# Attention with a feed-forward branch, float32, one core: a new order of each unit's work on TensorE, ScalarE and VectorE

## Chip, core and metric

The kernel runs on one core of a Trainium2 chip. The metric is the device time of one execution in microseconds, as a median of several. The engines are called by their short names in the rows: PE (TensorE; PEld is its weight load), ACT (ScalarE), DVE (VectorE), POOL (GpSimd) and SP (SyncE, which issues all DMAs here).

## What is computed

The input x is (4, 1024, 128) in float32. With xn the layer norm of x over the last axis, the result is x + attention(xn) + ffn(xn).

```python
# attention
xq, xk, xv = rope(xn @ Wq), rope(xn @ Wk), xn @ Wv      # 16 heads of 64; k and v have 512 columns
xk, xv = jnp.repeat(xk, 2, axis=-1), jnp.repeat(xv, 2, axis=-1)
scores = softmax(xq @ xk * scale, axis=-1)              # scale = (64 / 16) ** -0.5
out = (scores @ xv) @ Wo
# ffn
h = silu(xn @ wg.T) * (xn @ wu.T)                       # 384 hidden, integer weights / 127
out = h @ wd.T
```

Since each column of k and v is repeated, a head has 32 different ones (E = 32). The projection weights are drawn eight times larger than usual, so the scores are large and the softmax needs its row maximum.

## The kernel before

**Units.** A step is one batch and one group of four heads (16 steps, s), with a half of the 1024 queries as a unit: 32 units, u = 2s + t. Unit u computes 8 key tiles (kt) of 128 keys against 512 queries for 4 heads (h). The body `slot` (L544 on PE, L847 on ACT, L1051 on DVE, L1191 on POOL) is written out for units 0 to 30; the last unit has code of its own (`last_slot`). Units 28 to 30 (`last_pair`) project nothing any more.

**What one unit does.** All engines run their own list in order and meet at semaphores.

- Scores (`score`, L551 to 556): 32 matmuls, one for each kt and h, from `qk_pack` into `bank_s`, which has two places, by h % 2. ACT takes the exponential of each (L867) into `prob`, a ring of 4 key tiles. The row maximum is subtracted by two extra rows of `qk_pack` (98 rows instead of 96), so a unit's maxima must be known before it begins. Score (kt, h) waits until the exponential two scores back is done.
- Maxima (`max_tile`, L386): for the next unit v = u + 1, 16 tiles m of 128 queries; each is two matmuls of 512 columns (queries against all 1024 keys) into one of two places of the tensor `scores` (m % 2), and one maximum on DVE (`reduce_tile`, L943, L946). Tile m waits until DVE has read tile m - 2. After tile 15 DVE splits the maxima into two parts (`split_max`, L952 and L954), PE transposes them (`transpose_max`, L398), ACT copies them (`read_maxT`, L764), and SP's DMA (`pack_max`, L252) puts them into `qk_pack`; the next unit's first score waits for that (L582).
- V products (`pv`, L400 to L408): for each kt eight instructions in the profile, into four column strips of 32 of the array (`bank_o`). Before, they come in pairs of key tiles (`pv_pair`, L558): kt 6 and 7 of the unit before, then 0 and 1, 2 and 3, 4 and 5.
- Denominators: POOL adds the eight exponential tiles (L1173, L1181; tiles 4 and 5 are first added on DVE, `pair_sum`, L1039). PE sums over keys with a matrix of ones, also in column strips (`denominators`, L416 and L419), ACT copies (`read_den`, L834), PE transposes (`transpose_den`, L426), DVE inverts (`invert`, L1043), ACT spreads (`spread_inv`, L839), PE transposes back (`transpose_inv`, L433), DVE multiplies (`normalise`, L1049). All of it is for unit u - 1, and `project_out` (L442) for unit u - 2; `read_o` (L828) and `read_y` (L845) copy results out of PSUM.
- Projections for unit u + 4: four chunks c for q and k (`project`, L373, three matmuls each, into the same tensor `scores`; `project_chunk` waits for maxima that have been read) and V (`project_v`, L381, twelve matmuls into `bank_m`). DVE rotates the chunks (`rotate`, L937 to L941, six instructions); ACT rounds (`round_hi`, L753) and copies V (`stage_v`, L758); POOL takes the remainder (`split_lo`, L1125); SP packs heads with 24 DMAs a step (`pack_heads`, L239) and V with two (`pack_v`, L247), all in even units.

`bank_m` holds in turn the transposed maxima, V, the output product, the denominators and both transposes.

**The order around the change.** The order is written by hand in PE's `slot`: for each kt the scores h = 0 to 3 and between them the other work. `maxima()` takes the next tile of an iterator. On ACT the copies stand behind given exponentials (kt, h). On DVE `INVERT_AFTER` says after which maximum the inversion comes; the normalisation stands behind the split.

Of the kernel before, what the change touches and what calls it, by code (L numbers as in the profile page):

```python
# [39 lines left out]
UNITS = 2 * STEPS  # L40
HALF = S // 2

KT = S // 128
# [28 lines left out]
INVERT_AFTER = 9  # L72


def build(nc, x, tables, w_qkv, wo_even, wo_odd, w_gu, w_down, ident_in, out):
# [10 lines left out]
    with ctx:  # L86
# [272 lines left out]
        def _(pe):  # L359
# [184 lines left out]
            def slot(i, j, t, last_pair):  # L544
# [3 lines left out]
                do_max = not (last_pair and j == 1 and t == 1)  # L548
                tiles = iter(range(TILES))
# [8 lines left out]
                def pv_pair(kt):  # L558

                    if kt > 0:  # L560
                        pv(u, kt - 2, j)
                        pv(u, kt - 1, j)
                    elif not is_first(u):
                        pv(u - 1, KT - 2, j if t == 1 else 1 - j)
                        pv(u - 1, KT - 1, j if t == 1 else 1 - j)

                def maxima():
                    if do_max:
                        m = next(tiles)
                        if m < 2:  # L570

                            pe.wait_ge(rope_done, capped(2 * u + 7 + m, 2 * UNITS))
                        max_tile(v, m, v_n, v_t)
# [12 lines left out]
                if do_max and t == 1:  # L586

                    pe.wait_ge(packed, 16 * PACKS * (s + 1))
                for kt in range(KT):
                    score(kt, 0)  # L590
                    if kt == 0:
                        maxima()
                        score(kt, 1)
                        maxima()
                        score(kt, 2)
                        pv_pair(kt)
                        score(kt, 3)
                        maxima()
                    elif kt == 1:
                        maxima()  # L600
                        score(kt, 1)
                        if not is_second(u):
                            project_out(u - 2, 1 - j, s - 1)
                        score(kt, 2)
                        maxima()
                        score(kt, 3)
                    elif kt == 2:
                        maxima()
                        score(kt, 1)
                        maxima()  # L610
                        pv_pair(kt)
# [3 lines left out]
                        maxima()  # L615
                        score(kt, 3)
                        maxima()
                    elif kt == 3:
                        if not is_first(u):
                            transpose_den(u - 1)  # L620
                        score(kt, 1)
                        maxima()
                        score(kt, 2)
                        maxima()
                        score(kt, 3)
                    elif kt == 4:
                        maxima()
# [638 lines left out]
```

## Time and profile before

| | us |
|---|---|
| median of 3 runs | 1166.23 |
| the three runs | 1156.73, 1166.23, 1166.93 |
| the profiled execution | 1166.15 |
| its span, first to last instruction | 1164.4 |
| PE busy | 1120.0 (96%) |
| POOL busy | 852.9 (73%) |
| DVE busy | 901.1 (77%) |
| ACT busy | 729.8 (63%) |

The span is divided so: 110.7 us before the first unit, 31 units in the written-out body up to 1124.4, and the last unit. Matmuls are pipelined, so the recorded length of one is longer than what it takes of PE's time: the spacing from start to start tells that. A busy PE may thus be one that waits.

### The profile page before, as it was taken

The numbers are of one execution on the slowest core, as the hardware profiler recorded it, in microseconds if no ns is written. First come the engines' busy times: TensorE is split into PE (matmuls) and PEld (weight loads), VectorE is DVE, ScalarE is ACT, GpSimd is POOL, SyncE is SP. The second block draws the span as 40 slices with busy tenths as digits, with TensorE's granted clock in tenths as the row PEclk, the third lists the DMA queues.
The fourth block names the chain that finished last, engine by engine and source line by source line (L and its number), as shares of the span: only waits on it lengthen the run. The fifth ranks groups of instructions, "written<-read, shape, count | busy, mean of one in ns | idle before, by whom it ended". The sixth has DMA issues, their size and how long they took to land.

```text
span 1164.4 us, 17086 instructions
## 1 busy us (share of the span) xinstructions
PE 1120.0 (96%) x6288; PEld 663.2 (57%) x6288; DVE 901.1 (77%) x1023; ACT 729.8 (63%) x1327; POOL 852.9 (73%) x268
## 2 busy tenths in 40 slices
PE   5899899999999999999999999999999999999997
PEld 4787455655565555556565555555555555554443
DVE  7686877787887877788787877778787877776655
ACT  3234666666676666666676666666676666665564
POOL 3222868788788778888788778887778878887660
PEclk9899999999999999999999999999999999998889
DMA  6662908062340718062341718072341618050000
GB/s 230 159 258 77 256 2 224 1 205 58 85 141 19 207 37 224 2 205 57 96 129 26 201 37 224 1 210 53 96 130 30 196 37 224 1 130 1 5 1 19
DMA packets 56338, 124.98 MB, mean 107 GB/s; under 512 B 8000, under 2 KB 19520, under 8 KB 54080
## 3 DMA queue, kind: packets, MB, share of 16 engines
q1 hardware_dynamic: 56256, 123.90, 36.8%
q8 instruction: 51, 0.84, 0.3%
q14 instruction: 31, 0.25, 0.1%
HBM read 53.08 MB, written 10.49 MB: 55 GB/s over the span
## 4 chain that ended last, share of the span: by engine, by line
PE 79%; DVE 14%; SPq 2%; ACT 2%; issue 1%; DMA 1%; POOL 0%; DVEq 0%; ACTq 0%; POOLq 0%
PE bank_o L406 20%; PE bank_s L554 18%; PE scores L391 17%; DVE row_max L946 12%; PE scores L373 7%; PE bank_m L381 3%; PE bank_m L442 2%; PE bank_m L416 2%; PE bank_m L419 2%; SPq L239 2%; PE scores L492 2%; PE bank_s L509 1%; ACT prob L867 1%; PE bank_o L509 1%; DVE stats L961 1%
## 5 line engine op out<-in xcount | busy, mean ns | idle before, releaser
L946 DVE TENSOR_REDUCE row_max<-scores 128x1 f32<-128x1024 f32 x512 | 597.1, 1214 | 206.8 <-PE scores L391 206.5
L867 ACT ACTIVATE prob<-bank_s 128x512 f32<-128x512 f32 x992 | 576.7, 600 | 252.9 <-PE bank_s L554 229.5
L1181 POOL TENSOR_TENSOR prob_sum<-prob_sum,prob 128x2048 f32<-128x2048 f32 x93 | 425.7, 4577 | 13.5 <-ACT prob L867 0.5
L554 PE MATMUL bank_s<-qk_pack 98*128 98x512 f32 x992 | 415.8, 434 | 7.1 <-ACT prob L867 3.1
L391 PE MATMUL scores<-qk_pack 96*128 96x512 f32 x1024 | 337.5, 411 | 8.9 <-DVE row_max L946 0.3
L554 PEld LDWEIGHTS bank_s<-qk_pack 98*128 98x128 f32 x992 | 186.9, 189 | 184.9 <-issue 84.7
L406 PE MATMUL bank_o<-prob,v 128*32 128x512 f32 x2048 | 253.0, 612 | 0.0
L391 PEld LDWEIGHTS scores<-qk_pack 96*128 96x128 f32 x1024 | 179.5, 190 | 74.5 <-DVE row_max L946 53.0
L1181 POOL TENSOR_TENSOR prob_sum<-prob_sum,prob_pair 128x2048 f32<-128x2048 f32 x31 | 142.7, 4602 | 101.7 <-DVE prob_pair L1039 101.7
L1125 POOL TENSOR_TENSOR qk_stage<-rope,qk_stage 128x512 fp32r<-128x512 f32 x64 | 81.8, 1279 | 92.3 <-ACT qk_stage L753 92.3
L1173 POOL TENSOR_TENSOR prob_sum<-prob 128x2048 f32<-128x2048 f32 x31 | 142.2, 4586 | 0.0
L406 PEld LDWEIGHTS bank_o<-prob,v 128*32 128x32 f32 x2048 | 54.0, 110 | 123.1 <-issue 69.1
L373 PE MATMUL scores<-x_stage,w_stage 128*128 128x512 f32 x336 | 98.6, 401 | 0.0
L834 ACT COPY den<-bank_m 128x512 f32<-128x512 f32 x31 | 18.2, 586 | 86.6 <-PE bank_m L419 86.6
L1039 DVE TENSOR_TENSOR prob_pair<-prob 128x2048 f32<-128x2048 f32 x31 | 70.8, 2285 | 0.0
L373 PEld LDWEIGHTS scores<-x_stage,w_stage 128*128 128x128 f32 x336 | 61.4, 189 | 14.5
L1189 POOL TENSOR_TENSOR y_acc<-y_part,y_acc 128x512 f32<-128x512 f32 x31 | 39.5, 1274 | 26.5 <-ACT y_part L845 26.5
L381 PEld LDWEIGHTS bank_m<-w_stage,x_stage 128*128 128x128 f32 x336 | 46.3, 191 | 3.6
L937 DVE TENSOR_TENSOR scores<-scores,table 128x512 f32<-128x512 f32 x64 | 44.2, 691 | 2.5 <-PE scores L373 2.5
L941 DVE TENSOR_TENSOR rope<-scores,rope 128x512 f32<-128x512 f32 x64 | 44.3, 692 | 2.2
L939 DVE TENSOR_TENSOR rope<-scores,table 128x512 f32<-128x512 f32 x64 | 43.6, 681 | 0.6 <-PE scores L373 0.5
L381 PE MATMUL bank_m<-w_stage,x_stage 128*128 128x128 f32 x336 | 43.8, 266 | 0.0
(105 smaller groups left out, 742.4 us busy)
## 6 DMA issues: line engine op xcount, KB each, us to landing
qk_pack<-qk_stage SPq DMA_DIRECT2D x384, 128.0 KB, 5.0
table<-tables SPq DMA_DIRECT2D x16, 2048.0 KB, 9.6
w_stage<-w_scratch SPq DMA_DIRECT2D x14, 640.0 KB, 4.5
v<-v_stage SPq DMA_DIRECT2D x32, 256.0 KB, 8.1
xT_scratch<-xT_hl SPq DMA_DIRECT2D x4, 1024.0 KB, 9.5
x_stage<-xT_scratch SPq DMA_DIRECT2D x4, 1024.0 KB, 7.0
w_scratch<-w_split SPq DMA_DIRECT2D x1, 2560.0 KB, 15.1
x_all<-x SPq DMA_DIRECT2D x4, 512.0 KB, 11.7
```

The lines of the kernel that those rows point to most:

```text
L373: last = mm(scores[:, c, :], w_from[:, a, c, :], x_from[:, r, cols], start=n == 0, stop=n == 2)
L381: last = mm(bank_m[:, j * 128:(j + 1) * 128], x_from[:, r, at:at + 128], w_from[:, a, 4, :], start=n == 0, stop=n == 2)
L391: last = mm(scores[:, 2 * (m % places) + c, :], qk_pack[n][0:SPLIT_K, 0, t, h, (m % QT) * 128:(m % QT + 1) * 128], qk_pack[n][0:SPLIT_K, 1 ...
L406: last = mm(bank_o[h * E:(h + 1) * E, :], v_sb[n][:, kt, h * E:(h + 1) * E], prob[:, kt % RING, h, :], start=kt == 0, stop=kt == KT - 1)
L554: mm(bank_s[:, h % 2, :], qk_pack[j][0:SCORE_K, 1, kt // QT, h, (kt % QT) * 128:(kt % QT + 1) * 128], qk_pack[j][0:SCORE_K, 0, t, h, :], s ...
L867: A(prob[:, kt % RING, h, :], bank_s[:, h % 2, :], ACT.Exp).then_inc(prob_ready, 1)
L941: V.tensor_tensor(rope[:, 2 * k, :], scores[:, 2 * k, :], rope[:, 2 * k + 1, :], ALU.add).then_inc(rope_done, 1)
L946: V.tensor_reduce(row_max[:, m:m + 1], scores[:, at:at + 2, :].rearrange("p c k -> p (c k)"), axis=AX.X, op=ALU.max).then_inc(max_read, 1)
L1039: V.tensor_tensor(prob_pair[:], prob[:, 4 % RING], prob[:, 5 % RING], ALU.add).then_inc(pair_done, 1)
L1125: TT(qk_stage[:, 2 * k + 1, t, :], rope[:, 2 * k, :], qk_stage[:, 2 * k, t, :].bitcast(F32), ALU.subtract).then_inc(lo_done, 1)
L1173: TT(prob_sum[:, t], prob[:, 0], prob[:, 1], ALU.add).then_inc(sum_done, 1)
L1181: TT(prob_sum[:, t], prob_sum[:, t], part, ALU.add).then_inc(sum_done, 1)
```

## The change

The order of a unit is rewritten on PE, and the lists of ACT and DVE are set to suit. No matmul, exponential or maximum is added or left out.

- Maximum 0 of the next unit moves to the end of the present one (`next_first_maximum`), with the wait for the packed heads in front of it (`packed`, once in two units) and a wait for the rotation. The wait for `packed` at the head of odd units goes. The other 15 maxima have places named by number.
- The V products come as: kt 7 of the unit before (in kt 1), 0 and 1 together (kt 3), 2 (kt 4), 3 (kt 5), 4 to 6 together (kt 7). The denominators no longer follow a V product.
- `project_v` of unit u + 4: blocks 0 and 1 at the end of unit u, blocks 2 and 3 in kt 0 of unit u + 1 (`second_half_v`).
- The four chunks stand one between two scores in kt 6, and `transpose_max` behind them; it was between the first two.
- On ACT `round_hi`, `stage_v`, `read_o`, `read_den`, `spread_inv` and `read_maxT` move to other exponentials. On DVE the inversion comes after maximum 7 (before: 9) and the normalisation after maximum 14 (before: behind the split).
- The removed `do_max` was always true in the written-out body.

```diff
-INVERT_AFTER = 9
+INVERT_AFTER = 7
+NORMALISE_AFTER = 14
...
-                def pv_pair(kt):
-
-                    if kt > 0:
-                        pv(u, kt - 2, j)
-                        pv(u, kt - 1, j)
-                    elif not is_first(u):
-                        pv(u - 1, KT - 2, j if t == 1 else 1 - j)
+                def pv_last():
+                    if not is_first(u):
                         pv(u - 1, KT - 1, j if t == 1 else 1 - j)
...
+                def maximum(m):
+                    if m == 1:
+
+                        pe.wait_ge(rope_done, capped(2 * u + 8, 2 * UNITS))
+                    max_tile(v, m, v_n, v_t)
+
+                def next_first_maximum():
+                    if u + 2 <= LAST:
+
+                        pe.wait_ge(rope_done, capped(2 * u + 9, 2 * UNITS))
+                        if t == 0:
+                            pe.wait_ge(packed, 16 * PACKS * (s + 1))
+                        max_tile(u + 2, 0, 1 - j, t)
+
+                def second_half_v():
+                    if 1 <= u <= UNITS - 4:
+                        project_v(u + 3, 1 - t, blocks=range(QT // 2, QT))
...
-                if do_max and t == 1:
-
-                    pe.wait_ge(packed, 16 * PACKS * (s + 1))
                 for kt in range(KT):
                     score(kt, 0)
                     if kt == 0:
-                        maxima()
+                        if is_first(u):
+                            pe.wait_ge(rope_done, 7)
+                            max_tile(v, 0, v_n, v_t)
+                        maximum(1)
                         score(kt, 1)
-                        maxima()
+                        second_half_v()
                         score(kt, 2)
-                        pv_pair(kt)
+                        maximum(2)
                         score(kt, 3)
-                        maxima()
+                        maximum(3)
                     elif kt == 1:
-                        maxima()
+                        pv_last()
+                        maximum(4)
                         score(kt, 1)
+                        maximum(5)
+                        score(kt, 2)
                         if not is_second(u):
                             project_out(u - 2, 1 - j, s - 1)
-                        score(kt, 2)
-                        maxima()
                         score(kt, 3)
+                        maximum(6)
                     elif kt == 2:
-                        maxima()
+                        maximum(7)
                         score(kt, 1)
-                        maxima()
-                        pv_pair(kt)
                         if not is_first(u):
                             denominators(u - 1, 1 - t)
                         score(kt, 2)
-                        maxima()
                         score(kt, 3)
-                        maxima()
-                    elif kt == 3:
+                        maximum(8)
                         if not is_first(u):
                             transpose_den(u - 1)
+                        maximum(9)
+                    elif kt == 3:
                         score(kt, 1)
-                        maxima()
+                        pv(u, 0, j)
+                        pv(u, 1, j)
                         score(kt, 2)
-                        maxima()
                         score(kt, 3)
+                        maximum(10)
+                        maximum(11)
                     elif kt == 4:
-                        maxima()
                         score(kt, 1)
-                        pv_pair(kt)
+                        pv(u, 2, j)
                         score(kt, 2)
-                        maxima()
+                        maximum(12)
                         score(kt, 3)
-                        maxima()
+                        maximum(13)
                     elif kt == 5:
                         if not is_first(u):
                             transpose_inv(u - 1)
                         score(kt, 1)
-                        maxima()
+                        maximum(14)
                         score(kt, 2)
-                        maxima()
+                        pv(u, 3, j)
                         score(kt, 3)
+                        maximum(15)
                     elif kt == 6:
-                        pv_pair(kt)
+                        project_chunk(0)
                         score(kt, 1)
-                        project_chunk(0)
+                        project_chunk(1)
                         score(kt, 2)
...
-                        project_chunk(1)
+                        project_chunk(2)
                         score(kt, 3)
-                        project_chunk(2)
+                        project_chunk(3)
+
+                        at_least(pe, o_done, u)
+                        transpose_max(v)
                     else:
-                        project_chunk(3)
                         score(kt, 1)
+                        for n in (4, 5, 6):
+                            pv(u, n, j)
+                        score(kt, 2)
+                        score(kt, 3)
+                        next_first_maximum()
                         if not last_pair:
                             pe.wait_ge(maxT_read, v + 1)
                             project_v(w, t, blocks=range(QT // 2))
-                        score(kt, 2)
-                        if not last_pair:
-                            project_v(w, t, blocks=range(QT // 2, QT))
-                        score(kt, 3)
...
                     if kt == 1:
-                        pv(LAST - 1, KT - 2, 1)
                         pv(LAST - 1, KT - 1, 1)
...
-                        if (kt, h) == (0, 2) and not first and staged:
+                        if (kt, h) == (0, 2) and staged:
+                            round_hi(0, u + 3, 1 - t, s + 1 + t)
+                        elif (kt, h) == (1, 0) and not first and staged:
                             stage_v(u + 3, 1 - t, s + 1 + t)
-                        elif (kt, h) == (0, 3) and not first:
+                        elif (kt, h) == (1, 1) and not first:
                             read_o(u - 1)
-                        elif (kt, h) == (1, 1) and staged:
-                            round_hi(0, u + 3, 1 - t, s + 1 + t)
-                        elif (kt, h) == (1, 3) and not is_second(u):
-                            read_y(u - 2)
-                        elif (kt, h) == (2, 1):
+                        elif (kt, h) == (1, 3):
+                            if not is_second(u):
+                                read_y(u - 2)
                             if staged:
                                 round_hi(1, u + 3, 1 - t, s + 1 + t)
-                            if not first:
-                                read_den(u - 1)
-                        elif (kt, h) == (4, 1) and not first:
+                        elif (kt, h) == (2, 1) and not first:
+                            read_den(u - 1)
+                        elif (kt, h) == (2, 3) and not first:
                             spread_inv(u - 1)
-                        elif (kt, h) == (6, 2) and not (last_pair and j == 1 and t == 1):
+                        elif (kt, h) == (6, 3):
                             read_maxT(u + 1)
...
-                    split_max(u + 1)
-                else:
-                    invert(u - 1)
-                if not is_first(u):
-                    normalise(u - 1)
+                for m in range(TILES):
+                    reduce_tile(u + 1, m)
+                    if m == INVERT_AFTER and not is_first(u):
+                        invert(u - 1)
+                    if m == NORMALISE_AFTER and not is_first(u):
+                        normalise(u - 1)
+                split_max(u + 1)
                 pair_sum(u)
```

## Rows read from the trace of the kernel before

**Rows 1.** The page: busy time, share of the span, instructions.
```profile
PE 1120.0 (96%) x6288; PEld 663.2 (57%) x6288; DVE 901.1 (77%) x1023; ACT 729.8 (63%) x1327; POOL 852.9 (73%) x268
```

**Rows 2.** Busy time by stretches: start:end, length, each engine's busy time, PE's granted clock.
```profile
143.10:177.00 33.90, 33.09 (x177) 18.12 (x177) 25.30 (x27) 20.98 (x38) 23.41 (x7) 0.95 0.01 2
177.00:1026.10 849.10, 841.68 (x4812) 490.06 (x4811) 684.19 (x702) 569.45 (x1040) 693.00 (x209) 1.00 0.38 108
1026.10:1124.00 97.90, 94.73 (x484) 47.98 (x483) 67.50 (x65) 62.16 (x114) 73.30 (x21) 0.93 0.16 40
...
568.72:601.36 32.64, 32.35 (x186) 18.83 (x186) 26.33 (x28) 21.91 (x40) 26.69 (x9) 1.00 0.72 200
```

**Rows 3.** Who waited for whom, 177 to 1026.1: total us, times, longest us.
```profile
PEld bank_s L554 <- ACT prob L867: 51.5, 130, 0.8
PEld scores L391 <- DVE row_max L946: 44.1, 104, 0.6
```

**Rows 4.** The chain of waits in order of time, 600 to 670: start, us, what.
```profile
603.16 0.24 PE bank_s L554
603.40 1.85 PE bank_o L406 x16
605.25 0.43 PE bank_s L554
605.68 0.47 PE scores L391 x2
...
608.68 0.71 PE bank_s L554 x2
...
612.59 0.86 PE bank_m L416 x8
...
628.51 0.70 PE scores L373 x3
...
629.45 0.21 PE bank_m L398
...
634.02 0.63 PE bank_s L554 x2
```

**Rows 5.** PE's timeline, 617 to 619: start, us, line, operation.
```profile
617.12 0.39 PE L554 MATMUL bank_s<-qk_pack 98*128 98x512 f32 x1
617.65 0.74 PE L391 MATMUL scores<-qk_pack 96*128 96x512 f32 x2
618.23 0.63 PE L554 MATMUL bank_s<-qk_pack 98*128 98x512 f32 x2
```

**Rows 6.** DVE's timeline, 596 to 634.
```profile
598.44 0.69 DVE L937 TENSOR_TENSOR scores<-scores,table 128x512 f32<-128x512 f32 x1
...
602.34 2.35 DVE L946 TENSOR_REDUCE row_max<-scores 128x1 f32<-128x1024 f32 x2
...
622.61 4.62 DVE L946 TENSOR_REDUCE row_max<-scores 128x1 f32<-128x1024 f32 x4 [1.52 <-PE scores L391]
627.27 0.86 DVE L952 CAST max_hl<-row_max 128x16 fp32r<-128x16 f32 x1
```

**Rows 7.** ACT's timeline, 596 to 634.
```profile
618.67 1.79 ACT L867 ACTIVATE prob<-bank_s 128x512 f32<-128x512 f32 x3 [0.53 <-PE bank_s L554]
...
626.03 1.09 ACT L867 ACTIVATE prob<-bank_s 128x512 f32<-128x512 f32 x2 [0.51 <-PE bank_s L554]
```

**Rows 8.** POOL's timeline, 596 to 634.
```profile
611.60 1.28 POOL L1125 TENSOR_TENSOR qk_stage<-rope,qk_stage 128x512 fp32r<-128x512 f32 x1 [1.96 <-ACT qk_stage L753]
...
618.80 9.30 POOL L1181 TENSOR_TENSOR prob_sum<-prob_sum,prob 128x2048 f32<-128x2048 f32 x2
```

**Rows 9.** SP's timeline in unit 14 (from 568.72), and L247's DMAs there.
```profile
590.53 0.60 SPq L247 DMA_DIRECT2D v<-v_stage  x1
...
DMA to landing us min/median/max: 5.7/7.7/9.8
```

**Rows 10.** Stretches at the seam of units 28 and 29 (columns as in rows 2).
```profile
1057.00:1060.50 3.50, 3.50 (x12) 2.25 (x15) 1.86 (x2) 2.01 (x4) 3.50 (x1) 0.50 0.02 5
```

More of the change, by code:

```diff
@@ L547, in slot @@
                 v_n, v_t = (j, 1) if t == 0 else (1 - j, 0)
-                do_max = not (last_pair and j == 1 and t == 1)
-                tiles = iter(range(TILES))
                 def score(kt, h):
@@ L556, in score @@
                        qk_pack[j][0:SCORE_K, 0, t, h, :], start=True, stop=True).then_inc(score_ready, 1)
-                def pv_pair(kt):
-                    if kt > 0:
-                        pv(u, kt - 2, j)
-                        pv(u, kt - 1, j)
-                    elif not is_first(u):
-                        pv(u - 1, KT - 2, j if t == 1 else 1 - j)
-                        pv(u - 1, KT - 1, j if t == 1 else 1 - j)
[L567 to L573, printed above, removed]
+                def pv_last():
+                    if not is_first(u):
+                        pv(u - 1, KT - 1, j if t == 1 else 1 - j)
+                def maximum(m):
[11 more added lines that the diff above has]
+                        project_v(u + 3, 1 - t, blocks=range(QT // 2, QT))
                 def project_chunk(c):
@@ L637, in slot @@
                         score(kt, 1)
-                        maxima()
+                        maximum(14)
                         score(kt, 2)
-                        maxima()
+                        pv(u, 3, j)
                         score(kt, 3)
+                        maximum(15)
                     elif kt == 6:
-                        pv_pair(kt)
+                        project_chunk(0)
                         score(kt, 1)
-                        project_chunk(0)
+                        project_chunk(1)
                         score(kt, 2)
-                        if do_max:
-                            at_least(pe, o_done, u)
-                            transpose_max(v)
-                        project_chunk(1)
+                        project_chunk(2)
                         score(kt, 3)
-                        project_chunk(2)
+                        project_chunk(3)
+                        at_least(pe, o_done, u)
+                        transpose_max(v)
                     else:
-                        project_chunk(3)
                         score(kt, 1)
+                        for n in (4, 5, 6):
[3 more added lines that the diff above has]
+                        next_first_maximum()
                         if not last_pair:
@@ L1052, in slot @@
                 u = 4 * i + 2 * j + t
-                do_max = not (last_pair and j == 1 and t == 1)
-                if do_max:
-                    for m in range(TILES):
-                        reduce_tile(u + 1, m)
-                        if m == INVERT_AFTER and not is_first(u):
-                            invert(u - 1)
-                    split_max(u + 1)
-                else:
-                    invert(u - 1)
-                if not is_first(u):
-                    normalise(u - 1)
+                for m in range(TILES):
[5 more added lines that the diff above has]
+                split_max(u + 1)
                 pair_sum(u)
```

## Prediction

> **What bounds the kernel now.** I read four views in this order. The page's busy times name PE, 96% busy, as the bound; no other engine is over 77% [rows 1]. Busy time by stretches says where the span goes: 26 regular units take 849.1 us, 32.66 each, at full clock; one taken alone is 32.64 [rows 2]. A busy PE may still wait, so the third view is who waited for whom: in these 26 units PE's weight loads waited 51.5 us for ACT and 44.1 us for DVE, 3.7 us a unit, partly hidden behind the matmul before [rows 3]. What is not hidden I took from PE's list of starts. Undisturbed steps are: a score 0.23 us (0.24 at 603.16), a maximum 0.47, eight instructions in column strips 0.86, a chunk 0.70 [rows 4]. Where a step takes longer, PE waited or switched. Two patterns are seen in the rows. The score before the third maximum in a row (617.12) is followed after 0.53 instead of 0.23, and that maximum itself takes 0.58 instead of 0.47 [rows 5]: DVE takes 1.15 a tile (four in 4.62 [rows 6]) and PE only 0.94 for two scores and a maximum. This happens twice a unit, 0.82 in all. Two scores in a row behind the output product take 0.71 instead of 0.47 [rows 4], because a score waits for the exponential two before. Taking the undisturbed lengths away from all 68 steps of a unit, 15 places stay late, by 1.85 us together. So 32.64 = 30.79 of work and switches + 1.85 of waits.
>
> **Work on PE: added.** Each group of V products costs more than its instructions. From the score before it to the maximum behind it, 603.16 to 605.68, are 2.52 us: 0.24 + 1.85 + 0.43 [rows 4]. Two scores and sixteen instructions at the denominators' pace of 0.86 for eight would be 2.19. So a group costs 0.33 for its two changes. Before, a unit has four such groups, the second with the denominators in it. Now it has six: kt 7 of the unit before; the denominators; 0 and 1; 2; 3; 4 to 6. Two more make +0.67. A group of a single product is not in the trace. It costs nothing extra if the price hangs on the weight loads alone, and at most twice 0.33 if each neighbour pays in full; 0 to 1.3 for two more. I take 0.33, the price of the groups that are there. All other steps keep number, length and kind of neighbour. Work without a wait: 30.79 + 0.67 = 31.46.
>
> The Trainium skill bears on this: TensorEngine Tiling (Array Packing), Key Properties, says that changing the tiling mode drains the engine. By that rule each change between whole-array matmuls and 32-column strips costs again, however short the group, which speaks against this change; the trace has 0.33 for a group's two changes. The rule gives no figure and so no sum of its own.
>
> **Waits on PE: walked through with the durations of before.** Rules, each from rows: an exponential starts 0.44 us after its score (618.23 to 618.67; put at 0.54 behind V products), takes 0.60, and the next one begins 0.5 after it (two in 1.09) [rows 5, 7]; a tile's reduction starts 0.65 after its maximum and takes 1.15 [rows 6]. Starts in the new order, from the unit's first score: m1 0.28, score (0,1) 0.75, V 0.98, (0,2) 1.60, m2 1.89, m3 2.59, (1,0) 3.05, product 7 3.37, m4 4.34, m5 5.14, output product 5.84, (1,3) 6.65, m6 6.97, m7 7.67, (2,1) 8.13, denominators 8.45, (2,2) 10.30, m8 10.88, transpose 11.34, m9 11.70, (3,0) 12.25, products 0 and 1 12.80, (3,2) 14.65, m10 15.23, m11 15.69, (4,0) 16.16, (4,1) 16.39, product 2 16.71, m12 18.02, m13 18.72, back-transpose 19.42, m14 20.09, product 3 20.88, m15 22.19, chunks 22.89 to 26.37, maxima transposed 26.37, (7,0) 26.48, products 4 to 6 27.03, (7,2) 29.75, next m0 30.32, V 30.78, end 31.4.
>
> - Maxima against DVE: at most two stand together, then 2 to 5 us of other work. The closest are m14 (tile 12 read at 19.9, needed 20.09) and m5 (4.9 against 5.14). The pattern of 0.82 goes.
> - Scores against ACT: the closest is (4,1) at 16.39, its exponential ending at 16.30. About 0.1.
> - Denominators against `read_y`: copied at 8.2, needed at 8.45. About 0.05.
> - DVE's inversion: it moves behind tile 7, and the transposed denominators come at 11.95, 2 us after tile 7 is read. Tile 8 (maximum at 10.88) waits for it until 12.2. Tile 10 doesn't need it before 15.2: hidden.
> - `round_hi` second half, `read_y` and then POOL: remainder at 8.8 (before 10.2: 611.60 in a unit from 601.36 [rows 8]), output addition 10.0, first addition 11.3, the third ends at 25.3.
> - `split_max`: tile 15 is read at 24.05, but before, the 16-column conversion took 0.86 and ended when POOL's addition ended (627.27 + 0.86 = 628.13 against 618.80 + 9.30 = 628.10 [rows 6, 8]). So it ends at 25.35, not 24.2. Transposing at 26.37 still has 0.8 in hand. Behind it on DVE stand the pair sum (2.2) and the rotation, 3.9 (598.44 to 602.34 [rows 6]): done at 31.6. The next unit's m1 needs it at 31.4 + 0.28 = 31.68. Nothing in hand; I put 0.05.
> - The packed maxima: before, the transposition stood at 629.45 and the next unit's first score at about 634.2, 4.7 us later and without a wait for the DMA [rows 4]; now 26.37 to 31.4, 5.0.
> - m0 at 30.32 waits in even units for the packed heads. In unit 14 the last DMA went out at 590.53, 21.8 into the unit, and landed 5.7 later at 27.5 [rows 9]. SP starts a step's packing when V of unit u + 4 is complete, now 1.6 us later; so 29.1, 1.2 in hand.
>
> Waits left: 0.2 of 1.85 (ends: 0 and all 1.85). A regular unit: 31.46 + 0.2 = 31.66, 0.98 less; 26 units: -25.5 us.
>
> SBUF — State Buffer in the Trainium skill (Who interferes with whom) says that a DVE cast in a two-port mode and a POOL instruction lock each other out for a whole instruction. By that rule, the trace agrees (0.86 us, ending with the addition). Without that rule the conversion would end at 24.2 and the end of the rotation be 1.1 us earlier.
>
> **Ends of the run.** Unit 0 must wait at its end for packed heads as before, and m0 and V now come after that: +1. Unit 1 (33.9, with PE for a time at half clock, 0.95 on average [rows 2]) has the same half clock, no output product and fewer waits: -1.5. Units 28 to 30 took 97.9 at a mean of 0.93 of the clock [rows 2]. They project nothing, so kt 6 and 7 were a sparse row of eight scores at the pace of ACT, and behind it PE ran at 0.50, 1.2 GHz, V products doubled [rows 10]. Now V products 4 to 6 stand in it: walked through, a unit is 29.6 at full clock, 88.8 for three, up to 5.4 more if the clock falls at both seams as before (2.7 each: 33.6 against 30.9). I take 92: -6. The last unit has one product fewer at its start: -1. Together -7.5.
>
> Sum: the profiled execution took 1166.15 (span 1164.4 and 1.75 around it); less 25.5 and 7.5 gives 1133.1. The median of the runs is 1166.23, the same base. Forecast: **1133 us**.
>
> **Rivals.**
>
> 1. *DVE's tail becomes the bound.* The chain from POOL's third addition over conversion, pair sum and rotation to the next m1 has no slack in the walk. For: POOL is 82% busy in these units [rows 2], and the conversion waits for it. Against: POOL starts 1.4 us earlier than before. If POOL's additions run 0.6 later than walked, m1 comes 0.5 to 0.6 late in every unit: 1133 + 26 x 0.5 = 1146.
> 2. *PE's waits go elsewhere, or short groups cost double.* For: no wait for DVE was over 0.6 us [rows 3], and such small ones my walk can miss; no single product is in the trace. Against: the walk, applied to the order of before, meets the waits that are there. Price: 0.67 for groups and 0.3 of waits, 1.0 a unit, all of the gain: 1133 + 26 = 1159. This is also the case in which the change doesn't do what it says.
> 3. *m0 waits for the packed heads, on the slow side.* The wait is now at 30.3 of an even unit instead of at the next unit's start, and packing starts 1.6 later. V's DMAs took 5.7 to 9.8 us to land [rows 9]. At 9.8 the last would land at 33.2, and PE, with V, the next unit's scores and m1 queued behind the wait, stands for 2.9 us in 13 units: 37 us. Unit 1 followed such a stop and had 0.95 of the clock over 33.9 us, 1.7 us lost [rows 2]: 22 more. 1133 + 59 = 1192. It decides from a wait of 2 us alone, which eats the gain of two units, and from a few tenths where the 1.7 of the clock come with it. Against: the 5.7 is the last one's own.
>
> TensorE: Matmul & The Clock Gate in the Trainium skill (What's actually happening) says that the throttled clock is the default and activity releases it. By that rule rival 3's second term follows each long stop; the rows agree in unit 1 and at units 29 and 30.
>
> **How the numbers follow.** Chances: forecast 0.63 (its own range 1122 to 1142, from switches and waits 0.35 us a unit either way), rival 1 0.16, rival 2 0.13, rival 3 0.08. Range 1120 to 1158: rivals 1 and most of 2 are in, 3 is left out with a little of 2. A measurement can tell about 1%, 12 us. Faster by over 1% (under 1154.5): the forecast, rival 1 and a third of 2, 0.83. Within 1%: the rest of 2, 0.09. Slower: rival 3, 0.08.
>
> **What would show it.** Right: 26 regular units of 31.5 to 31.8; PE's weight loads for maxima waiting for DVE almost nowhere; six groups of strips at 0.33 each; the third addition ending near 25.3 and the conversion with it; units 28 to 30 in 89 to 94. Wrong: a maximum 1 late behind the rotation every unit (rival 1), starts beside single products over 0.4 apart (rival 2), or a gap before maximum 0 in even units with half clock behind it (rival 3).

## The result, and the profile after

The changed kernel took 1128.22 us (median of four runs, 1127.29 to 1129.61) against 1165.34 before, a ratio of 0.970, 95% interval 0.965 to 0.974: 3% faster. The forecast was 1133. Its profiled execution took 1127.29 with a span of 1125.4.

The line of busy times on the page of the changed kernel, against [rows 1]:

```profile
PE 1090.5 (97%) x6288; PEld 661.9 (59%) x6288; DVE 912.1 (81%) x1023; ACT 722.1 (64%) x1327; POOL 853.3 (76%) x268
```

The instructions are the same in number. What went is PE's time. Busy time by stretches (start:end, length, PE, PEld, DVE, ACT, POOL, granted clock, DMA share, GB/s): unit 0, unit 1, the 26 regular units, units 28 to 30, the last unit.

```profile
109.55:141.87 32.32, 28.82 (x141) 15.90 (x142) 26.05 (x26) 20.39 (x36) 26.62 (x9) 1.00 0.82 243
141.87:173.41 31.54, 31.50 (x180) 17.91 (x179) 25.89 (x28) 21.19 (x39) 24.22 (x7) 1.00 0.01 2
173.41:995.80 822.39, 822.39 (x4812) 492.97 (x4812) 694.90 (x702) 563.61 (x1040) 692.84 (x208) 1.00 0.39 112
995.80:1087.84 92.04, 89.38 (x489) 45.93 (x489) 67.11 (x64) 61.13 (x114) 75.90 (x22) 0.98 0.17 43
1087.84:1125.40 37.56, 28.81 (x176) 13.07 (x176) 18.52 (x19) 19.82 (x39) 7.04 (x3) 0.88 0.05 15
```

The last unit of the kernel before, for comparison:

```profile
1124.40:1164.40 40.00, 31.17 (x184) 14.04 (x184) 18.52 (x19) 20.14 (x39) 9.94 (x4) 0.84 0.05 14
```

A regular unit is 822.39 / 26 = 31.63 us, where it was 32.66 [rows 2]: 26.7 us of the 39.0 by which the span shrank. The other 12.3 came at the ends: 6.3 in units 28 to 30 (98.3 before, counted to the last unit's first score), 2.4 each in unit 1 and the last unit, 1.1 ahead of the first.

The chain of waits in order of time shows a regular unit of the changed kernel (584.6 to 616.2); its lines answer to [rows 4, 5]:

```profile
597.54 1.85 PE bank_o L407 x16
599.39 0.66 PE bank_s L553 x2
600.05 0.91 PE scores L392 x4
600.96 0.54 PE bank_s L553 x2
601.50 1.00 PE bank_o L407 x8
602.49 0.43 PE bank_s L553
...
610.64 0.71 PE scores L374 x3
611.35 0.11 PE bank_m L399
611.46 0.47 PE bank_s L553 x2
611.92 2.71 PE bank_o L407 x24
```

Four matmuls of maxima (two tiles) take 0.91, scores 0.23: the steps of 0.53 and 0.58 [rows 5] and of 0.71 for two scores [rows 4] are gone. DVE is in this chain no more. A single V product takes 1.00 and the score behind it 0.43. Set against 0.86 for eight instructions and 0.24 for a score, that is 0.14 ahead and 0.19 behind, 0.33 for the group; the groups of two (1.85) and of three (2.71) pay the same 0.13 and 0.19, once each. Only at 600.96 do two scores take 0.54 instead of 0.47, at the place where the walk had put 0.1.

Who waited for whom in the 26 regular units, 173.41 to 995.80, against [rows 3]; and the weight loader's timeline at the one place of a unit where it waits for DVE:

```profile
PEld bank_s L553 <- ACT prob L871: 93.1, 130, 0.8
PEld scores L392 <- DVE row_max L950: 21.8, 26, 0.8
```

```profile
588.95 0.30 PEld L392 LDWEIGHTS scores<-qk_pack 96*128 96x128 f32 x2 [0.84 <-DVE row_max L950]
```

The waits for DVE are half of what they were (44.1), and there is one a unit where there were four. The one that is left stands behind the V product in kt 1. Behind each of the six groups the weight loader shows the same 0.84 idle, whether the view names DVE (588.95), ACT (599.32) or only "issue" (614.56): it is the time in which PE runs the group, and belongs to the group's price. So the waits for DVE that PE felt are gone, and the total for ACT could rise from 51.5 to 93.1 in a faster kernel. The starts of matmuls, not this view, tell what a wait costs.

DVE's and POOL's timelines at the end of the same unit:

```profile
608.91 1.13 DVE L956 CAST max_hl<-row_max 128x16 fp32r<-128x16 f32 x1
...
615.61 0.69 DVE L945 TENSOR_TENSOR rope<-scores,rope 128x512 f32<-128x512 f32 x1
```

```profile
600.67 9.34 POOL L1181 TENSOR_TENSOR prob_sum<-prob_sum,prob 128x2048 f32<-128x2048 f32 x2
```

The conversion of 16 columns takes 1.13 us and ends at 610.04, the addition at 610.01. The rotation ends at 616.30, 0.10 into the next unit (616.20), and maximum 1 stands at 0.28. The chain of the first rival is there and just misses PE.

### The profile page after: what moved, and what is told of

The parts are those of the page before. It is cut to its first block, busy times and chain, and to the rows that moved or that the text cites. A ratio compares the mean times of both kernels' runs of the same rounds, so it can differ in the third digit from the quotient of the medians.

```text
span 1125.4 us, 17086 instructions
## 1 busy us (share of the span) xinstructions
PE 1090.5 (97%) x6288; PEld 661.9 (59%) x6288; DVE 912.1 (81%) x1023; ACT 722.1 (64%) x1327; POOL 853.3 (76%) x268
## 4 chain that ended last, share of the span: by engine, by line
PE 93%; DVE 4%; ACT 2%; DMA 1%; issue 1%; ACTq 0%; DVEq 0%
PE bank_s L553 24%; PE scores L392 22%; PE bank_o L407 21%; PE scores L374 8%; PE bank_m L382 3%; PE bank_m L417 3%; PE bank_m L420 2%; PE bank_m L443 2%; PE scores L493 2%; PE bank_s L510 1%; PE bank_m L427 1%; PE bank_m L434 1%; DVE row_max L950 1%; PE bank_o L510 1%; PE bank_m L510 1%
## 5 line engine op out<-in xcount | busy, mean ns | idle before, releaser
L871 ACT ACTIVATE prob<-bank_s 128x512 f32<-128x512 f32 x992 | 566.2, 599 | 274.0 <-PE bank_s L553 263.9
L553 PE MATMUL bank_s<-qk_pack 98*128 98x512 f32 x992 | 393.4, 427 | 3.4 <-ACT prob L871 2.0
L392 PE MATMUL scores<-qk_pack 96*128 96x512 f32 x1024 | 323.4, 402 | 2.4 <-DVE rope L945 1.7
L553 PEld LDWEIGHTS bank_s<-qk_pack 98*128 98x128 f32 x992 | 178.2, 188 | 176.2 <-ACT prob L871 117.5
L392 PEld LDWEIGHTS scores<-qk_pack 96*128 96x128 f32 x1024 | 184.6, 189 | 61.1 <-DVE row_max L950 28.8
L407 PEld LDWEIGHTS bank_o<-prob,v 128*32 128x32 f32 x2048 | 50.5, 109 | 112.4 <-issue 89.4
L374 PEld LDWEIGHTS scores<-x_stage,w_stage 128*128 128x128 f32 x336 | 63.7, 190 | 14.7
L1047 DVE RECIPROCAL den_inv<-bank_m 128x16 f32<-128x16 f32 x31 | 8.0, 258 | 60.5 <-PE bank_m L427 60.5
```

What stands on the lines that cost most here:

```text
L374: last = mm(scores[:, c, :], w_from[:, a, c, :], x_from[:, r, cols], start=n == 0, stop=n == 2)
L392: last = mm(scores[:, 2 * (m % places) + c, :], qk_pack[n][0:SPLIT_K, 0, t, h, (m % QT) * 128:(m % QT + 1) * 128], qk_pack[n][0:SPLIT_K, 1 ...
L407: last = mm(bank_o[h * E:(h + 1) * E, :], v_sb[n][:, kt, h * E:(h + 1) * E], prob[:, kt % RING, h, :], start=kt == 0, stop=kt == KT - 1)
L553: mm(bank_s[:, h % 2, :], qk_pack[j][0:SCORE_K, 1, kt // QT, h, (kt % QT) * 128:(kt % QT + 1) * 128], qk_pack[j][0:SCORE_K, 0, t, h, :], s ...
L871: A(prob[:, kt % RING, h, :], bank_s[:, h % 2, :], ACT.Exp).then_inc(prob_ready, 1)
```

## The experiments

Each starts from the changed kernel. "Regular unit" is its 26 units' stretch over 26, to be set against 31.63. That length is the sharp measure, since the whole varies by several us from one execution to the next (below); the first nine edits were executed once each. Where an edit leaves these units alone, their length came out at 31.62 and 31.63 again.

**A seventh group.**

```diff
 pv(u, 0, j)
-pv(u, 1, j)
 score(kt, 2)
+pv(u, 1, j)
 score(kt, 3)
```

> The changed kernel, with V products 0 and 1 on either side of score (3,2) instead of together: a seventh group of column strips, nothing else. Theory A (PE is the bound, and each group costs 0.33 us for its two changes, also a single one): a regular unit goes from 31.63 to 31.97, the whole by 31 x 0.34 = 10.5, about 1138. Theory B (the price hangs on the weight loads, whose number doesn't change): 31.63 and 1127 to 1129. If single products cost double, 32.3 and 1149.

Measured: 1138.0, regular unit 31.93. Stretch, and chain of waits:

```profile
174.41:1004.62 830.21, 830.21 (x4812) 489.76 (x4812) 689.62 (x703) 566.32 (x1040) 692.91 (x208) 1.00 0.39 111
```

```profile
570.53 0.99 PE bank_o L407 x8
571.52 0.43 PE bank_s L553
571.96 1.00 PE bank_o L407 x8
```

Two singles and the two scores behind them take 0.99 + 0.43 + 1.00 + 0.43 = 2.85 us; in the changed kernel the group of two and the same scores take 1.85 + 0.66 = 2.51 (597.54 and 599.39 above). That is 0.34 for one more group, and the unit grew by 0.30, since score (4,1) waits less. A group costs the same whatever its length: theory A, and the term of the prediction.

**Normalisation late.**

```diff
-                    if m == NORMALISE_AFTER and not is_first(u):
-                        normalise(u - 1)
                 split_max(u + 1)
+                if not is_first(u):
+                    normalise(u - 1)
```

> The changed kernel, with DVE's normalisation behind the split of the maxima again, as before the change. Theory A (POOL's third addition, the conversion that ends with it, pair sum and rotation are a chain that ends just ahead of maximum 1; it has some 0.15 us in hand): 0.6 us more on it make maximum 1 wait 0.45 in every unit with a rotation, a regular unit 32.1, the whole about 1140. Theory B (DVE, 81% busy, has slack wherever it works): 31.63, no change.

Measured: 1150.5, regular unit 32.20. Stretch, and PE's timeline at the seam of two units:

```profile
174.59:1011.81 837.22, 830.11 (x4813) 489.56 (x4812) 695.19 (x702) 563.17 (x1040) 692.14 (x209) 1.00 0.39 110
```

```profile
560.55 0.44 PE L553 MATMUL bank_s<-qk_pack 98*128 98x512 f32 x1
561.29 0.73 PE L392 MATMUL scores<-qk_pack 96*128 96x512 f32 x2 [0.29 <-DVE rope L945]
561.86 0.39 PE L553 MATMUL bank_s<-qk_pack 98*128 98x512 f32 x1
```

Maximum 1 starts 0.74 behind the first score, not 0.28, released by the rotation, and itself takes 0.57: 0.46 + 0.10. Its weight load, which else runs ahead, starts together with it (561.29). Theory A, a little larger than written (32.1). Of the 23 us in the whole, 15 are these units; the rest came at the ends, which were not taken apart.

**V at the end.**

```diff
-                        second_half_v()
...
-                            project_v(w, t, blocks=range(QT // 2))
+                            project_v(w, t)
```

> The changed kernel, with V of unit u + 4 projected whole at the end of unit u, nothing in kt 0. Theory A: score (0,2) then stands 0.99 us behind score (0,0) where its exponential needs about 1.15, so PE waits 0.15 to 0.25 there and gains nothing elsewhere: a regular unit 31.8 to 31.9, the whole about 1133. Theory B (the half V only shifts work): 31.63, no change. Theory C (the half V in kt 0 is where much of the 1.0 us a unit came from): 32.1 or more.

Measured: 1138.1, regular unit 32.02. Stretch, and PE's timeline at the start of a unit (559.00):

```profile
174.73:1007.32 832.59, 830.47 (x4812) 488.32 (x4812) 697.01 (x703) 564.40 (x1040) 692.30 (x208) 1.00 0.39 110
```

```profile
559.74 0.97 PE L553 MATMUL bank_s<-qk_pack 98*128 98x512 f32 x2
560.54 0.64 PE L392 MATMUL scores<-qk_pack 96*128 96x512 f32 x2
```

Scores (0,1) and (0,2) take 0.80 together instead of 0.47, the expected wait with its bare load, 0.33; a little more at maximum 3. It costs 0.39: between theories A and C. The place of the half V is worth more than I had put.

**Both edits.**

> Both edits of the two runs before together. Theory A: with V whole at the end, the next unit's maximum 1 stands 0.6 us later against DVE's chain, so the late normalisation hides there: the unit is as long as with V at the end alone, within 0.1, and not 0.45 longer. Theory B (the late normalisation costs through another path, as the transposed maxima waiting for it): the two costs add up.

Measured: 1144.4, regular unit 32.17 (836.47 for the 26).

The late normalisation costs 0.57 alone and 0.15 here. With V in front of the unit's first score, maximum 1 is 0.6 later against DVE, and most of the chain's delay is hidden: in this run the rotation ends at 561.81, as the unit's first score starts (561.80), and maximum 1 follows at 562.09, 0.29 behind it, without a wait. The 0.15 are more than the 0.1 of theory A. Most of it stands at maximum 3, which takes 0.65 in the chain of waits (564.22) and not 0.53 as with V at the end alone; DVE begins its tiles later here. A delay that nearly vanishes when maximum 1 moves is what a single path, POOL's addition to maximum 1, does, and what two independent costs don't.

**Maximum 0 back in the next unit.**

```diff
-                        maximum(1)
+                        max_tile(v, 0, v_n, v_t)
                         score(kt, 1)
+                        maximum(1)
                         second_half_v()
...
-                        next_first_maximum()
```

(with the waits for rotation and packing ahead of maximum 0)

> The changed kernel, with maximum 0 back behind the next unit's first score, its waits with it, and maximum 1 behind the second. Theory A (PE is the bound and DVE has 5 us of idle time a unit): DVE starts its maxima about 0.9 later but catches up in its gaps, PE waits 0.1 or less: a regular unit 31.6 to 31.75, no change that counts; unit 0's end loses its wait ahead of maximum 0 and unit 1's start gets it. Theory B (the early start of the maxima is what lets each have other work beside it): 32.0 or more, the whole 1137 or more.

Measured: 1143.7, regular unit 32.15. Stretch, PE's timeline and DVE's at the start of a unit (558.02):

```profile
172.24:1008.02 835.78, 832.19 (x4812) 493.19 (x4811) 695.31 (x702) 566.51 (x1041) 693.24 (x209) 1.00 0.39 110
```

```profile
560.87 0.40 PE L553 MATMUL bank_s<-qk_pack 98*128 98x512 f32 x1
561.41 0.73 PE L392 MATMUL scores<-qk_pack 96*128 96x512 f32 x2
```

```profile
559.00 4.62 DVE L950 TENSOR_REDUCE row_max<-scores 128x1 f32<-128x1024 f32 x4 [0.51 <-PE scores L392]
```

Theory A fell; the length is that of theory B. DVE's rotation was done at 558.5 but its first tile came at 559.00; four tiles then ran without a gap and PE stood 0.54 instead of 0.23 ahead of maximum 3, which took 0.57. With 0.09 where the first score, without maximum 0 ahead of it, waits for its exponential, that makes 0.5. DVE's 5 us of idle time lie elsewhere in the unit and didn't help here, where the maxima come in a bunch.

**Three maxima in a row.**

```diff
-                        if not is_first(u):
-                            transpose_inv(u - 1)
                         score(kt, 1)
                         maximum(14)
+                        if not is_first(u):
+                            transpose_inv(u - 1)
```

> The changed kernel, with the back-transpose of the denominators behind maximum 14 instead of ahead of score (5,1), so that maxima 12, 13 and 14 have only scores between them. Theory A (that pattern was the largest wait of the kernel before, 0.41 each): maximum 14 comes 0.4 late and the next step 0.1 more; a regular unit 32.1, the whole about 1142. Theory B (PE makes up for it later, since DVE is free then): 31.7 or less.

Measured: 1143.2, regular unit 32.02. Stretch, and PE's timeline:

```profile
177.21:1009.80 832.59, 832.59 (x4813) 491.58 (x4812) 687.48 (x703) 560.50 (x1040) 692.57 (x208) 1.00 0.39 110
```

```profile
580.66 0.88 PE L553 MATMUL bank_s<-qk_pack 98*128 98x512 f32 x2
581.44 0.73 PE L392 MATMUL scores<-qk_pack 96*128 96x512 f32 x2
582.01 0.60 PE L434 MATMUL bank_m<-ident,den 128*128 128x128 f32 x4
```

Two scores take 0.78 (0.47 undisturbed) and the maximum 0.57, 0.41 in these steps and 0.39 in the unit: the price of one such place, of which the kernel before had two. Theory A. The transposition, 0.36 us long here, is worth about its own length as something to do between maxima.

**Five groups.**

```diff
 pv(u, 2, j)
+pv(u, 3, j)
...
-                        pv(u, 3, j)
+                        maximum(15)
                         score(kt, 3)
-                        maximum(15)
```

> The changed kernel, with V product 3 beside product 2 in kt 4 and maximum 15 moved ahead of score (5,3): five groups instead of six. Theory A (a group costs 0.34, but without the single product as a filler scores wait for exponentials and maximum 15 and the first chunk for DVE, some 0.3 to 0.6): 31.6 to 31.9, nothing won. Theory B (fewer groups is what counts): 31.3 or less, the whole about 1117.

Measured: 1138.5, regular unit 31.86:

```profile
175.41:1003.69 828.28, 824.78 (x4813) 493.10 (x4812) 678.13 (x703) 560.36 (x1040) 693.47 (x209) 1.00 0.39 111
```

```profile
579.25 0.40 PE L553 MATMUL bank_s<-qk_pack 98*128 98x512 f32 x1
579.78 0.73 PE L392 MATMUL scores<-qk_pack 96*128 96x512 f32 x2
580.35 0.64 PE L553 MATMUL bank_s<-qk_pack 98*128 98x512 f32 x2
580.91 0.96 PE L374 MATMUL scores<-x_stage,w_stage 128*128 128x512 f32 x3
```

One group less, 0.34, and the waits are back: 0.53 instead of 0.23 ahead of maximum 15, which takes 0.57, 0.56 instead of 0.47 for the two scores behind it, and 0.80 instead of 0.70 for the first chunk, 0.59 together. Net 0.23 longer, theory A. The single V product pays for itself as something to do between scores.

**Filled ends.** In units 28 to 30, kt 6 and 7 become: score, product 4, two scores, product 5, score, transposition; score, next maximum 0, two scores, product 6, score.

> The changed kernel, with units 28 to 30 (no projections) rearranged at their end: V products 4, 5 and 6 and the next maximum 0 stand one by one between the scores of kt 6 and 7, which wait for exponentials there. Theory A: two more groups (0.68) against 1.7 to 2.2 us of waits a unit, and no sparse stretch behind which the clock falls: the three units take about 85.5 instead of 92.0, the clock stays at 1.00 until the last unit, the whole 1121. Theory B (ACT is the bound there, and the order on PE doesn't matter): 91 to 92, no change.

Measured: 1125.1, regular unit 31.62. Units 28 to 30, the last unit:

```profile
996.06:1083.80 87.74, 87.02 (x489) 44.88 (x489) 67.42 (x64) 60.93 (x113) 73.77 (x21) 1.00 0.18 45
1083.80:1123.40 39.60, 28.31 (x177) 12.56 (x176) 20.19 (x19) 20.07 (x39) 9.26 (x4) 0.92 0.05 14
```

```profile
ACT prob L929 <- POOL prob_sum L1195: 2.0, 1, 2.0
```

The three units take 4.3 us less at full clock (theory A had 6.5, theory B none), but the last one takes 2.0 more than in the changed kernel: half of it was given back. The clock isn't the reason, since the last unit's is higher here, 0.92 against 0.88. The third block (who waited for whom, 1083.80 to 1123.40) names it: ACT waits 2.0 us for POOL's last addition of unit 30, a wait that the changed kernel doesn't have. That addition ends at 1090.65, behind DVE's pair sum of 1079.00 and an addition before it, and at 1092.33 in the changed kernel. So POOL's tail came only 1.7 us earlier, and not 4.3.

**Packing late.**

```diff
-                    at_least(sp, score_ready, 64 * s)
+                    at_least(sp, score_ready, 64 * s + 8)
```

> The changed kernel, with SP starting the packing of heads in even units 8 scores later (about 6.7 us into the unit instead of 1.8). In the changed kernel's trace the last packed piece lands 0.7 to 3.3 us ahead of maximum 0. Theory A (the slow rival's mechanism, with a margin of some 1 to 3 us): the last lands 2 to 5 us later, maximum 0 waits 1 to 3 us in the 13 regular even units, the whole 1140 to 1165, more where the clock falls behind such a wait (1.7 us each). Theory B (the transfers are bound by the transfer of the tables and by the end of the remainder on POOL, not by their start): less than 1 us a wait, the whole under 1135.

Measured: 1241.7, regular unit 35.70. Stretches (all regular units; the 10 us behind a stop, at the seam of units 14 and 15), and PE's timeline there:

```profile
182.48:1110.66 928.18, 884.08 (x4812) 529.20 (x4812) 698.93 (x702) 566.24 (x1040) 692.16 (x208) 0.93 0.35 99
575.00:585.10 10.10, 10.10 (x34) 6.81 (x33) 4.90 (x4) 3.97 (x7) 3.77 (x2) 0.50 0.00 0
```

```profile
574.62 0.92 PE L392 MATMUL scores<-qk_pack 96*128 96x512 f32 x2 [3.62 <-issue]
```

The mechanism of the slow rival works, and worse than I wrote, a whole of 1140 to 1165 with waits of 1 to 3 us: PE stands 3.6 us ahead of maximum 0 (3.0 to 3.8 in the 13 units) with V and the next scores behind it, and then runs 10 us at 0.50, 1.2 GHz (7 to 10 behind each of the 13 such stops). The row names no releaser, but in each of them maximum 0 starts 0.09 us behind the landing of the last packed piece. A pair of units grows by 8.1 us, under half of which is the wait itself. In the changed kernel the last piece lands 0.7 to 3.3 us ahead of maximum 0 in units 2 to 26.

**The changed kernel again.**

> The changed kernel as it is, beside the next one on the same chip. All theories: 1127 to 1130, regular units 31.63, ratio to before 0.970.

Measured: 1132.5 (four runs, 1128.0 to 1136.7), ratio 0.974, interval 0.969 to 0.979. Units 0 and 1 of the execution of 1136.7:

```profile
111.24:181.85 70.61, 64.82 (x319) 36.78 (x319) 52.05 (x53) 41.72 (x75) 50.81 (x15) 0.93 0.40 112
```

The median is above the 1127 to 1130 that I expected; two of the four runs took 1136 and 1137. The 26 regular units agree to 0.1 us (822.33). Units 0 and 1 take 70.6 instead of 63.9: there the packed heads landed 33.3 us into unit 0, not 31.1, maximum 0 came right behind after a stop of 4.0 us, and the clock fell to half for 10 us. The slow rival is real in one unit, unit 0.

**Joined transposition, with the filled ends.**

```diff
-                        at_least(pe, o_done, u)
-                        transpose_max(v)
                     else:
                         score(kt, 1)
+                        at_least(pe, o_done, u)
+                        transpose_max(v)
                         for n in (4, 5, 6):
```

> The changed kernel with two edits: the end of units 28 to 30 as in the run with the filled ends, and in the other units the transposition of the maxima (a matmul in a 32-column strip) moved from behind the last chunk to just ahead of V products 4 to 6, so that it shares their change of tiling; ScalarE's copy of it goes behind exponential (7,1). Theory A (each change between whole-array and strip matmuls costs about 0.1 wherever it stands, and the packed maxima have over 1 us in hand): a regular unit 31.53 to 31.56, 2 to 3 us in all, with the ends 5 more: about 1121. Theory B (such a single small matmul hides its change): 31.63, and 1124.

Measured: 1129.9 (1126.1 to 1132.1), ratio 0.972, interval 0.969 to 0.976. Regular unit 31.65 (822.99 for the 26), no gain. The chain of waits:

```profile
584.93 0.70 PE scores L374 x3
585.63 0.49 PE bank_s L553 x2
586.12 0.11 PE bank_m L399
586.23 2.71 PE bank_o L407 x24
```

Theory A fell here; the regular unit is that of theory B, and the whole isn't told apart from the changed kernel's. From the start of the last chunk to the first V product are 1.30 us, and 1.28 in the changed kernel (610.64 to 611.92 above). The transposition takes 0.11 in both places, and in the changed kernel the two scores behind it take their usual 0.47, without the 0.19 that follows a group. A matmul of V's projection, 128 columns as well and with no change beside it, takes 0.10 (six in 0.62 at 615.75). So this single matmul paid next to nothing for a change, and there was nothing to save.

**Ends, once more.** The filled ends, and maximum 0 of unit 0's end moved behind V in unit 1's kt 0.

> The changed kernel with filled ends in units 28 to 30 (as in the run before) and maximum 0 of unit 1's list taken out of unit 0's end, where PE waits for the packed heads with V and the next scores behind it; it now stands behind V in unit 1's kt 0. Theory A (unit 0's wait for the packing, 2 to 6 us and half clock behind it, is what makes the changed kernel vary between 1127 and 1137): units 0 and 1 together take 62 to 64 us in every run instead of 63.9 to 70.6, the whole 1120 to 1125 with less spread. Theory B (the wait only moves by one score): 64 to 70, spread as before, 1123 to 1132.

Measured: 1127.2 (1126.4 to 1128.9), ratio 0.972, interval 0.966 to 0.977. Units 0 and 1, and the last:

```profile
109.60:173.73 64.13, 61.87 (x318) 34.79 (x319) 51.85 (x53) 41.95 (x75) 50.86 (x15) 0.97 0.42 123
1083.79:1124.60 40.81, 29.92 (x177) 13.21 (x176) 20.19 (x19) 20.10 (x39) 9.25 (x4) 0.85 0.05 14
```

The whole is within the noise of the changed kernel's 1128.2. Theory A had 1120 to 1125, and that fell. Units 0 and 1 are 64.1, about as written (62 to 64): the stop is gone, though the clock was at half for 3.4 us in unit 0 (112.6 to 116.0) all the same. The four runs lie within 2.5 us, but so did the four of the changed kernel beside the kernel before (2.3), and this doesn't show that the spread is gone. The 4.3 us won in units 28 to 30 (87.75 us again) came back as 3.3 in the last unit: 2.0 is the same wait of ACT for POOL as with the filled ends, and the clock was lower, 0.85 on average (0.88 in the changed kernel, 0.92 in the run with the filled ends). None of the versions beats the changed kernel by more than the noise.

## Why the prediction was right, point by point

- **Where the time was.** 1.85 us of waits in a unit of PE's: right. One of its two large places, put back, cost 0.39 of the 0.41 read from the list.
- **Groups of V products.** 0.33 each: right; for one more, of single products, 0.34 in its own steps and 0.30 net in the unit.
- **The signs.** The third addition and the conversion, the six groups and the 92.0 for units 28 to 30 came as written. The weight loads for maxima were to wait for DVE almost nowhere; they wait 21.8 us, once a unit. That row didn't come as written, though what I meant by it did, since the wait lies under a V product (588.95).
- **The walk.** 31.66 for a regular unit, 31.63 measured. The reach of single steps is as good: the conversion was to end at 25.35 and ended 25.45 into the unit, the rotation at 31.6 and 31.7, maximum 0 at 30.32 and 30.56, the wait at score (4,1) 0.1 and 0.07.
- **The rivals.** POOL's and DVE's tail has 0.15 to 0.2 us in hand; 0.6 more on it costs 0.57. Waits went nowhere else. Packed heads have 0.7 us or more in hand, save in unit 0. Rival 3 put 1.7 us of clock behind each stop; the late packing showed 4.7, the 8.1 of a pair less 3.4 of stop on average, so its price was too low.
- **The ends.** -7.5 predicted, -12.3 measured; this is the term that was mis-sized, and 4.8 of the 5.8 between 1133.1 and the 1127.3 of this execution (the regular units gave 26.7, and not 25.5). Units 28 to 30 gave 6.3 (6). Unit 0 lost nothing in that execution (I had +1), unit 1 gave 2.4 (1.5), since the clock didn't fall there, the last unit 2.4 (1), and the stretch ahead of unit 0, which the change doesn't touch, was 1.1 shorter. The run of 1136.7 shows the other side of unit 0: this part depends on when the DMAs land, and my +1 and half clock describe that run.
- **What had not been seen.** How strongly the parts hang together. Undoing one of four small moves (half V, maximum 0, the transposition between maxima, the early normalisation) gives back 0.39 to 0.57 of the 1.03 us each, 1.87 in sum. The gain belongs to the order as a whole, and can't be shared out among its parts. The places of the chunks, the earlier inversion and ScalarE's new places were not undone one by one; what each of them gives isn't shown.

The page TensorEngine Tiling (Array Packing) of the Trainium skill (Key Properties: a change of tiling mode drains the engine) is borne out for the V products by the run with a seventh group, at 0.34 us for a group's two changes. It is not for the single transposition, whose rows name a strip of 32 columns too (128*32): it took 0.11 us, next to no more than its own length, in either place.

## What to carry to other kernels

Where one engine is nearly always busy, take its list of starts and set each step against its undisturbed length: the sum of the excess is what an order can win, and walking the new order through with the other engines' durations tells which of it comes back. Work that must be done anyway is filler; a group split in two costs two changes of tiling more, 0.33 us here, and still pays where longer waits stood. At the end of a run, look at which engine's tail the last stage waits for, before giving the bound engine a better order there: of the 4.3 us won in units 28 to 30, 2.0 went into a wait for POOL. Before moving a wait earlier on the bound engine, read how far ahead of it the data land in every unit, the first above all: a stop of 3 to 4 us cost more than its own length again in clock.

## What the runs showed of the hardware

- A wait on PE costs more than its length: the maximum behind it took 0.57 instead of 0.47 in four different places (maxima 1, 3, 14 and 15 of four runs).
- Behind stops of 3 to 4 us PE ran 7 to 10 us at half clock, every time in the late-packing run. Shorter stops went either way: behind 2.45 us at the end of unit 0 of the kernel before came 3.4 us at half clock (145.0 to 148.4), and behind 1.7 us at the end of unit 0 of the changed kernel's first trace the clock stayed at 1.00.
- A DVE conversion of 128 x 16 elements takes as long as POOL's running addition has still to go, 1.13 us here, and 0.86 before [rows 6]. With no addition running it took 0.17 (1078.70 in the run with the filled ends).
